# Two attention layers: one pipeline over all batches in place of a projection stage and an attention stage

## What is computed

```
q, k, v = x @ Wq, x @ Wk, x @ Wv            # 16 heads of 8 channels
q, k    = rotary(q), rotary(k)
s       = (q @ k.T) / sqrt(8)               # 512 x 512
s      += alibi                             # first layer only: slope * 8 * min(key - query, 0)
out     = softmax(s) @ v
y       = concat(out) @ Wo + b
```

## Time and profile before

| | |
|---|---|
| median of 3 runs | 2182.98 us (2178.91 to 2183.33) |
| profiled execution, own time | 2180.4 us |
| its span in the profile | 2178.6 us |
| TensorE, VectorE, ScalarE, GpSimd busy | 1634.6, 1139.2, 872.1, 390.0 us |
| granted clock of TensorE, mean | 0.867 of 2.4 GHz |
| first attention layer | 8.7 to 379.9 us |
| fourth attention layer, without its layernorm | 1524.2 to 1835.7 us |

### The profile page before, as it was taken

One profiled execution on the slowest core, in us unless ns is written; L12 is line 12 of the kernel. 1 busy time (PEld: TensorE's weight loads), 2 busy tenths in 40 slices (PEclk: granted clock), 3 DMA queues, 4 the chain that ended last, 5 costly groups with the idle time before them and its releaser, 6 DMA issues. The chain is left out here.

```text
span 2178.6 us, 25289 instructions
## 1 busy us (share of the span) xinstructions
PE 1634.6 (75%) x8319; PEld 714.7 (33%) x8319; DVE 1139.2 (52%) x2326; ACT 872.1 (40%) x1220; POOL 390.0 (18%) x249
## 2 busy tenths in 40 slices
PE   4399998899659887577997500652489997779997
PEld 2044444333213332332343200651223322334443
DVE  7777772100039999254775392222588882533332
ACT  3155555422368874211666200111135655234333
POOL 4200000000059985000222005023400000000000
PEclk8599999899769999698999755785679998889998
DMA  3411110100000000001103400125501111000000
GB/s 106 97 22 26 22 22 1 53 0 0 21 4 5 4 4 0 26 0 31 40 21 137 184 0 6 31 34 50 145 15 24 30 23 56 36 5 0 0 0 19
DMA packets 52176, 70.90 MB, mean 33 GB/s; under 512 B 11172, under 2 KB 46092, under 8 KB 50204
## 3 DMA queue, kind: packets, MB, share of 16 engines
q1 hardware_dynamic: 50044, 67.36, 10.7%
q0 software_dynamic: 2048, 2.48, 1.7%
HBM read 47.81 MB, written 18.35 MB: 30 GB/s over the span
## 5 line engine op out<-in xcount | busy, mean ns | idle before, releaser
L614 ACT ACTIVATE a_probs_sb<-a_t_ps 128x1024 f32<-128x1024 f32 x256 | 262.2, 1024 | 283.3 <-PE a_t_ps L551 156.8
L530 PE MATMUL a_s_ps<-a_ks,a_qs 96*128 96x512 bf16 x512 | 213.2, 418 | 86.8 <-PEq L70 53.6
L648 DVE CUSTOM_DVE_ANT_0 a_biased<-a_s_ps,a_bias 128x512 f32<-128x512 f32 x256 | 169.1, 686 | 77.2 <-issue 67.1
L652 DVE TENSOR_REDUCE a_least_sb<-a_s_ps 128x1 f32<-128x512 f32 x256 | 167.8, 687 | 60.7 <-PE a_s_ps L530 59.4
L547 PE MATMUL a_t_ps<-a_qs,a_ks 126*128 126x512 bf16 (+1 forms) x512 | 195.1, 386 | 0.0
L1252 DVE TENSOR_TENSOR_SCAN s_h<-s_dA,s_dbu 128x1024 f32<-128x1024 f32 x64 | 146.6, 2290 | 52.1 <-POOL s_dbu L1217 44.3
L566 PE MATMUL a_o_ps<-a_probs_sb,a_vpad 128*32 128x256 f32 x2048 | 163.2, 391 | 4.7 <-ACT a_values_sb L622 2.1
L1217 POOL TENSOR_TENSOR s_dbu<-s_du,s_bs 128x1024 f32<-128x1024 f32 x64 | 152.3, 2391 | 27.8 <-DVE s_h L1252 27.3
L2576 DVE TENSOR_TENSOR c_gated_sb<-c_hid,c_g_ps 128x2048 f32<-128x2048 f32 x32 | 73.2, 2287 | 144.9 <-ACT c_hid L2566 144.9
L2566 ACT ACTIVATE c_hid<-c_up_ps,c_b 128x512 f32<-128x512 f32 x128 | 88.0, 687 | 142.1 <-PE c_up_ps L2535 142.1
L530 PEld LDWEIGHTS a_s_ps<-a_ks,a_qs 96*128 96x128 bf16 x512 | 49.9, 98 | 224.2 <-issue 70.7
(11 more groups left out here) (422 smaller groups left out, 2621.5 us busy)
## 6 DMA issues: line engine op xcount, KB each, us to landing
x_wu<-in_x_wu SPq DMA_DIRECT2D x2, 4096.0 KB, 16.9
a_stacks<-a_p SPq DMA_DIRECT2D x16, 384.0 KB, 3.7
a_qs<-a_stacks SPq DMA_DIRECT2D x32, 192.0 KB, 3.5
a_ks<-a_stacks SPq DMA_DIRECT2D x32, 192.0 KB, 3.9
a_stacks<-a_p SPq DMA_DIRECT2D x16, 256.0 KB, 3.3
q_q<-q_q SPq DMA_DIRECT2D x32, 128.0 KB, 2.3
x_wd<-in_x_wd SPq DMA_DIRECT2D x2, 2048.0 KB, 32.1
c_w<-in_c_w SPq DMA_DIRECT2D x2, 2048.0 KB, 10.4
```

Source lines behind the costliest of these rows:

```text
L530: nc.tensor.matmul(s_ps[n % 2][:, :], qs[0:LEAST_AT, h, t * P:(t + 1) * P], ks[0:LEAST_AT, h, :], start=True, stop=True).then_inc(scores_r ...
L614: nc.scalar.activation(probs[:, j % 4, :, :], t_ps[j % 2][:, :, :], ACT.Exp, scale=-1.0).then_inc(probs_ready, 1)
L648: nc.vector.tensor_tensor_reduce(out=biased[:, n % 2, :], in0=src, in1=bias[:, h, at:at + N], scale=1.0, scalar=3.0e38, op0=ALU.add, op1=A ...
L652: nc.vector.tensor_reduce(least[:, g % 2, n:n + 1], src, axis=AX.X, op=ALU.min).then_inc(least_ready, 1)
```

## The change

Projection and attention of a layer become one block, `attend`, written as one list of steps for all engines, unrolled. A step x is a tile of 128 queries for a pair of heads: 8 steps a group, 32 a batch, 128 in all. At step x the scores of x are made, the turned scores of step y = x - LAG (13 in the first layer, 14 in the fourth), and every second step the sums of values of the two steps before y - 1. What else TensorE does stands between the steps, at fixed places of a batch's 32: the four products of the next batch after steps 3 to 6, its values after 27, the turning of a group's least after 9, 17, 25 and (of the next batch) 1, the turning and normalising of a group's values after 24, 0, 8 and 16, the heads after 18, the output after 20. Only the products and values of batch 0 come before the steps.

- Scores have four PSUM banks (before two). Turned scores and all that stands between share three single banks in turn; the bank of a use is its number in a list modulo three.
- The exponential is per head, 512 columns (before 1024 for two).
- In the fourth layer one reduction takes the least of two heads at once (1024 columns); in the first it is one per head as before.
- The value sum is made over all 512 queries at once, with weights 16 columns wide (before 32) at the same four places, 32 partitions apart.
- ScalarE copies the turned least out of PSUM, and GpSimd splits it (before VectorE, out of PSUM).
- Normalising is per group of heads, not per tile of queries at the end of a batch.
- In the first layer ScalarE writes the alibi rows (before VectorE) and GpSimd the diagonal slopes (before VectorE).
- The subtraction after the high part and after the middle part is VectorE's for batch 0 and GpSimd's for the others.
- q and k stacks are one tile; semaphores of the layer are plain flags that count from 0.

```diff
-        if first:
-            project_and_split(core, A, xT, tag, stacks_dram, M, load_weights)
-        else:
+        if not first:
             layernorm_stage(core, xT, f"{tag}_ln", prefetch=load_weights)
-            project_and_split(core, A, xT, tag, stacks_dram, M, None)
-        attend(core, A, xT, tag, stacks_dram, M)
+        attend(core, A, xT, tag, M, alibi, load_weights if first else None)
...
+PROB_RING = 4
+SUM_LAG = 2
+RING_BANKS = 3
+PRODUCTS_AT = (3, 4, 5, 6)
+VALUES_AT = 27
+TURN_AT = (9, 17, 25, 1)
+NORM_AT = (24, 0, 8, 16)
+HEADS_AT = 18
+OUT_AT = 20
...
+        s_ps = core.ps(mem, f"{tag}_s_ps", [P, 4, N])
+        t_ps = core.ps(mem, f"{tag}_t_ps", [P, RING_BANKS, N])
+        o_ps = core.ps(mem, f"{tag}_o_ps", [P, N])
...
+        @block.sync
+            for i in range(B):
+                if i > 0:
+                    place(GROUPS * i - 1)
+                    load(GROUPS * i + 2)
+                if i + 1 < B:
+                    wait(sp, high, i + 2)
+                    store(i + 1, 0)
+                    wait(sp, middle, i + 2)
+                    store(i + 1, 1)
+                place(GROUPS * i)
+                if i > 0:
+                    load(GROUPS * i + 3)
+                if i + 1 < B:
+                    wait(sp, low, i + 2)
+                    store(i + 1, 2)
+                place(GROUPS * i + 1)
+                if i + 1 < B:
+                    load(GROUPS * (i + 1))
+                place(GROUPS * i + 2)
+                if i + 1 < B:
+                    load(GROUPS * (i + 1) + 1)
...
+        @block.tensor
+            def score(x, e):
...
+                if alibi:
+                    wait(pe, least_ready, 2 * x + e - 3)
+                elif e == 0:
+                    wait(pe, least_ready, x - 1)
...
+            def turned(y, e):
...
+                if u == 0 and e == 0:
+                    wait(pe, least_placed[k % 2], 16 * LEAST_ROWS * (k // 2 + 1))
...
+                free_bank("turned", y, e)
...
+            def sum_values(z):
...
+                for h in range(GROUP):
+                    y = 2 * z + h // 2
+                    last = nc.tensor.matmul(o_ps[h * VPAD:h * VPAD + VWIDE, :], vpad[:, i % 2, t, g * GROUP + h, :],
+                                            probs[:, y % PROB_RING, h % 2, :], start=(t == 0), stop=(t == KT - 1))
...
+            for x in range(TOTAL):
...
+                if x < ATT_STEPS:
+                    score(x, 0)
+                    if not alibi:
+                        score(x, 1)
+                if 0 <= y < ATT_STEPS:
+                    turned(y, 0)
+                if alibi and x < ATT_STEPS:
+                    score(x, 1)
+                if 0 <= y < ATT_STEPS:
+                    turned(y, 1)
+                if 0 <= z < ATT_STEPS and z % 2 == 1:
+                    sum_values(z // 2)
+                if s in between(i):
+                    make_between(i, s)
...
+        @block.scalar
+            if alibi:
+                wait(act, slopes_loaded, 16 * 5)
+                make_bias(0)
+            copy_high(0)
+            keep_v(0)
+            copy_middle(0)
+            if alibi:
+                for g in range(GROUPS):
+                    make_alibi(g)
+                    if g + 1 < GROUPS:
+                        make_bias(g + 1)
+            for x in range(TOTAL):
...
+                if x > 0 and before[1] in TURN_AT and before[1] in between(before[0]):
+                    keep_least(group_at(*before), bank("between", *before))
+                if 0 <= y < ATT_STEPS:
+                    exps(y, 0)
+                    exps(y, 1)
+                if 0 <= z < ATT_STEPS and z % GROUP_STEPS == GROUP_STEPS - 1:
+                    keep_values(z // GROUP_STEPS)
+                if i + 1 < B:
+                    if s == 8:
+                        copy_high(i + 1)
+                    if s == 11:
+                        copy_middle(i + 1)
+                    if s == VALUES_AT + 1:
+                        keep_v(i + 1)
+                if i > 0 and s == HEADS_AT + 1:
+                    wait(act, heads_turned, i)
+                    nc.scalar.activation(headsT[:, :], bank("between", i, HEADS_AT), ACT.Copy).then_inc(headsT_kept, 1)
...
+        @block.vector
+            nc.vector.memset(o_ps[:, :], 0.0).then_inc(sums_cleared, 1)
+            nc.vector.memset(stack[0:LEAST_AT, 0, :, :], 0.0).then_inc(q_cleared, 1)
+            if not alibi:
+                nc.vector.memset(stack[LEAST_AT:TURNED_ROWS, 1, :, :], -1.0).then_inc(minus_set, 1)
...
+        @block.gpsimd
+            for x in range(TOTAL):
+                i, s = divmod(x, BATCH_STEPS)
+                if s in TURN_AT and s in between(i):
+                    split_least(group_at(i, s))
+                if i + 1 < B:
+                    if s == 8:
+                        take_high(i + 1)
+                    if s == 11:
+                        take_middle(i + 1)
```

More of the change, by code:

```diff
@@ L302, in _ @@
-            for n in range(2):
-                sp.wait_ge(stored[n], START + 16 * STORES * B // 2)
+            wait(sp, q_cleared, 1)
+            wait(sp, k_cleared, 1)
+            wait(sp, high, 1)
+            store(0, 0)
+            wait(sp, middle, 1)
+            store(0, 1)
+            wait(sp, low, 1)
+            store(0, 2)
+            for g in range(GROUPS):
+                load(g)
+            for i in range(B):
+                if i > 0:
[7 more added lines that the diff above has]
+                place(GROUPS * i)
+                if i > 0:
+                    load(GROUPS * i + 3)
[8 more added lines that the diff above has]
+                    load(GROUPS * (i + 1) + 1)
@@ new lines, in turned @@
+            def turned(y, e):
+                k, u = divmod(y, GROUP_STEPS)
+                t, pair = divmod(u, 2)
+                h = GROUP * (k % GROUPS) + 2 * pair + e
+                out = bank("turned", y, e)
+                if y == 0 and e == 0 and not alibi:
+                    wait(pe, minus_set, 1)
+                if u == 0 and e == 0:
+                    wait(pe, least_placed[k % 2], 16 * LEAST_ROWS * (k // 2 + 1))
+                    if alibi and k < GROUPS:
+                        wait(pe, diag_ready, k + 1)
+                free_bank("turned", y, e)
+                last = nc.tensor.matmul(out, operand(1, k, pair, e, TURNED_ROWS)[:, t * P:(t + 1) * P],
+                                        operand(0, k, pair, e, TURNED_ROWS), start=True, stop=not alibi)
+                if alibi:
+                    for r in range(3):
+                        last = nc.tensor.matmul(out[:, t * P:(t + 1) * P], slopes_diag[:, r, h, :],
+                                                steps_table[:, :], start=False, stop=(r == 2))
+                last.then_inc(turned_ready, 1)
@@ L322, in _, with copy_high @@
         @block.scalar
         def _(act):
+            def copy_high(i):
+                wait(act, rotated, i + 1)
+                wait(act, stored, 16 * 6 * i)
+                nc.scalar.activation(parts[:, :, 0, :], prod[:, :, 0, :], ACT.Copy).then_inc(high, 1)
             def copy_middle(i):
[L325 to L329 removed]
@@ new lines, in _ @@
+            wait(dve, high, 1)
+            nc.vector.tensor_tensor(prod[:, :, 0, :], prod[:, :, 0, :], parts[:, :, 0, :],
+                                    ALU.subtract).then_inc(rest, 1)
+            wait(dve, middle, 1)
+            nc.vector.tensor_tensor(parts[:, :, 2, :], prod[:, :, 0, :], parts[:, :, 1, :],
+                                    ALU.subtract).then_inc(low, 1)
+            for x in range(TOTAL):
+                i, s = divmod(x, BATCH_STEPS)
+                if x < ATT_STEPS:
+                    least_of(x)
+                if s not in between(i):
+                    continue
+                if s in PRODUCTS_AT:
+                    rotate(i + 1, PRODUCTS_AT.index(s))
+                    if s == PRODUCTS_AT[-1]:
+                        add_products(i + 1)
+                if s in NORM_AT:
+                    normalise(group_at(i, s), bank("between", i, s))
+                if s == OUT_AT:
+                    add(i)
```

760 lines of the change are left out of this document (368 added, 392 removed).

## The result

The changed kernel took **2110.55 us** (median of 4 runs, 2107.59 to 2114.49), the kernel before 2183.15 beside it (2178.91 to 2183.69): ratio 0.9673, 95% interval 0.9651 to 0.9694. The forecast was 2100.0, range 2070 to 2138. The profiled execution took 2107.59 with a span of 2105.8, 72.8 us less than the profiled one of before; the forecast had 82.2.

What follows compares the result with a forecast made beforehand. TensorE was taken to bound the kernel. Gains of 35, 4.7, 4.4, 20, 11.7, 4.4 and 2 sum to 82.2 us; 2180.4 less that is 2098.2, plus 2.6 as a median gives 2100, range 2070 to 2138.

Steps and rivals of the forecast that it cites:

- First scores: First layer's prologue: only batch 0 is projected and stored before its scores, which begin at 38 us instead of 82.
- Score-only phase: First layer, 13 steps before turned scores: nine at 1.45 us, four with projections at 2.6, together 23.5 us.
- What is late next: First layer: ScalarE's alibi rows, casts and SP's queue delay turned scores to 71 us, before 106.0; gain 35.
- Steady step: First layer's steady phase: two halves of 0.61 us plus half a 1.09 us value sum, 1.765 us per step.
- First-group stalls: First group of batches 1 and 2: least rows land late, TensorE stalls 4 us each, 8 us per layer.
- It fits: Steady phase, first layer: the chain from small transpose to turned scores takes 5.4 us of 6.1 available.
- Fourth layer: Gains of 20 us up to the turned scores, 11.7 in the steady phase and 4.4 in the tail.
- 1: Rival: no stall at the first groups, stores and middle parts being ready sooner; 2084 us, chance 0.12.
- 2: Rival: value sums pack as by the span model, without the 0.14 fixed part; 2083 us, chance 0.04.
- 3: Rival: placing late in ordinary groups too and the clock falls in gaps, 34 us; 2134 us, chance 0.17.
- 4: Rival: three banks do not decouple, TensorE waits 1 us per in-between use, 88 us; 2188 us, chance 0.05.
- 5: Rival: value sums lose their packing with 16-column weights, 330 us slower; 2430 us, chance 0.04.

Runs made afterwards that it cites:

- e1: Changed kernel with GpSimd's slope products held back until the low parts of batch 0 are made; ratio 0.963 to the kernel before.
- c2: Changed kernel, slope products held back, least rows placed before stores, -1 rows later, last two groups' alibi rows spread over steps 13 to 28; 2063.2 us.
- e2: Changed kernel with SyncE placing a first group's least rows before storing the next batch's high and middle parts; ratio 0.9585 to the kernel before.
- c3: Changed kernel, slope products held back, least rows placed before stores, -1 rows later, heads and values copied ahead of the exponentials; 2065.0 us.
- r2: Changed kernel, slope products held back, least rows first, -1 rows later, alibi rows spread, copies ahead of exponentials, two banks in turn; 2109.7 us.
- e3: Changed kernel with the fourth layer's rows of -1 written after the low parts, not before VectorE's first product; ratio 0.9607 to the kernel before.

## Why the prediction was right, point by point

- **First scores.** Forecast at 38, measured 41.6. The step that failed is "multiply and add, cast, subtract": it left out VectorE's factor operations between the addition and the first subtraction, and that GpSimd's slope products run beside them, which cost 8 us. Without them (e1) the scores come 20.7 us after the projections; the forecast had 23.2. So its other terms were 2.5 us too dear, and that hid a third of the miss.
- **A rule that was not weighed.** The trace shows small VectorE operations that end when a GpSimd operation ends. The Trainium skill (SBUF — State Buffer, Who interferes with whom) says that the port pair shared by VectorE and GpSimd is held for a whole instruction, so that the second to come is blocked, not slowed. The trace agrees: 2.7 us instead of 0.25, each with its end at the end of a GpSimd product. It shows the other direction too: the product beside VectorE's addition took 3.73 us where the others take 2.75.
- **Score-only phase.** Step 13 was to be reached 23.5 us after the scores; c2 reaches it after 18.7. The step that failed is the price of 2.6 us for a step with a product, taken from TensorE at half clock. VectorE sets the pace there: two least in each step, 0.62 us from start to start, and for the next batch four multiplications of 0.69 and an addition of 1.23. An ordinary step takes 1.24 and the first three under 1.0, where the forecast had 1.45. In the first layer this changed nothing, since the first turned score waits for something else. In the fourth it is the 2 us by which that layer gave more (22.0 from the first score to the first turned one; the forecast had 23.7, and its own terms add up to 22.9).
- **What is late next.** That ScalarE's alibi rows and the casts behind them set the start of the turned scores was right (c2). ScalarE came to the cast at 64.7 instead of 61 to 62, and the turned scores start at 73.15 instead of 71. The queue of SyncE, also named, held back 0.45 us there (e2).
- **Steady step.** Right: 0.61 per half, 0.99 per value sum, 0.599 per exponential. The sum of work in the first layer, 244.5 us to the last value sum, compares with 244.4 to the last turned score, or 246.3 to the last value sum (c3 without its last wait). The agreement is in part luck, since the granted clock is still 0.50 in the first 4.6 us of that stretch of c3, which the sum doesn't have. The 0.13 of fixed part that the forecast kept is there in each of 128 sums. But it does not speak against the span model of the Trainium skill (TensorE: Matmul & The Clock Gate, Part 3), as the prediction took it to. That model is about how long a packed set lasts beside one matmul, and the prediction held it against a distance between starts. A product of 512 columns that is not packed, between the same neighbours, reads

```profile
186.10 1.08 PE L522 MATMUL a_t_ps<-xT,a_wqkv 128*128 128x512 f32 x2
```

(x2 since one such matmul leaves two records), and the next matmul starts at 187.02. So one matmul alone lasts 1.08 us and the packed set 1.05, and to the next start they take 0.92 and 0.99: at most 0.07 of the 0.13 belongs to the packing.
- **First-group stalls.** Right place and cause, 3.0 instead of 4 us; the heads 0.96 instead of 1.25. In the fourth layer they were 2.94 and 1.44, the heads cost nothing, and the values' copy, not named, took 1.02 three times: 7.4 us where 9 were forecast, which is in part luck.
- **What the sum lacked** in the first layer's steady phase: the lower clock behind the stalls (about 4.3 us, what e2 leaves over), and the last group's wait of 2.65. "It fits" held for ordinary groups only: the steps of the last group have no scores and are shorter. This is why 261.35 stands against 256.3.
- **Fourth layer.** 20, 11.7 and 4.4 against 22.2, 12.1 and 5.3. Its scores start 29.6 us after the projections, where 30 were forecast.
- **Barriers.** 2 against 1.9 is luck: no row priced them, and the 2 was the middle of a guess.
- **Stages between.** They were costed at nothing; 5.3 us went there in the profiled execution.
- **Rivals.** 1: wrong for the change, and what e2 makes of it (2090 where 2084 stood; the size is partly the clock, which the rival did not have). 2: its price is refuted by the 0.99 to the next start. 3: of the ordinary groups only the last of the first layer is late, but a fallen clock was real at the stalls. 4: refuted, with three banks TensorE waits for a copy only at the heads and the values (0.96 and 1.02, three times each); with two the loss is 53 us (r2), where the rival had 88. 5: refuted, 16 and 32 columns cost the same.

## What to carry to other kernels

When work moves to an idle engine, look at the instructions that run beside it: VectorE behind GpSimd lost more here than many operations cost. In a hand-written order of issues, what the bounding engine waits for goes ahead of what is only due a batch later, and a copy that frees a bank of the ring ahead of the work that needs the next. And a wait of 3 us costs more than 3 us when the clock falls behind it.

## What was not expected of the hardware

- A VectorE operation on 16 columns took 2.67 to 2.72 us beside GpSimd's products on SBUF and 0.23 to 0.29 alone; GpSimd's four took 11.86 us together and 10.89 when held back.
- After a wait of 3 us the granted clock was 0.50 for the next 6 us in one place (210 to 216) and 0.74 in a like one (138 to 144) of the same execution. In e3 the like place had 0.63 and, in the 6 us behind it, 0.80.
- The wait for the last group is not the shorter steps alone. Of its three placings one took 3.9 us to land, where others take 1.7, as the answer on the tile for 316 to 323 us says:

```profile
L383 SPq DMA_DIRECT2D a_stack<-a_least_parts x3: 502/590/590, 317.3 to 318.5; - x3
...
DMA to landing us min/median/max: 1.6/1.7/3.9
```

In e1 the same three landed in

```profile
DMA to landing us min/median/max: 1.6/1.7/1.7
```

and TensorE waited 0.49 us instead of 2.65. So some 2 us of this wait are the late landing. In the stretch of the changed kernel a packet of the queue that loads instructions is the only other traffic, and there is one in the stretch of e1 too. Whether it delays the placing wasn't tried.
- A memset of 3 rows at partition 96 takes 6.88 us on VectorE, with 1.76 us of idle time ahead of it in both places where it was tried.
